# Attention, residual and layer norm over 64 row tiles on one core: the order of six pieces of work in the last five tile pairs is changed

## The reference

```python
q = heads(x @ Wq + bq); k = heads(x @ Wk + bk); v = heads(x @ Wv + bv)
scores = einsum('bhqd,bhkd->bhqk', q, k) * scale
scores = where(mask == 0, -inf, scores)
out = einsum('bhqk,bhkd->bhqd', softmax(scores), v)
y = x + (out @ Wo + bo)
return (y - mean(y)) / sqrt(var(y) + 1e-5)
```

## Time and profile before

| what | us |
| --- | --- |
| median of 3 runs | 812.68 |
| lowest, highest | 810.5, 813.32 |
| the profiled execution | 811.64 |
| its span, first to last instruction | 809.5 |
| TensorE busy | 800.8 |
| VectorE busy | 642.8 |
| GpSimd busy | 551.4 |
| ScalarE busy | 267.1 |

### The profile page before, as it was taken

The page is one execution under the profiler, slowest core; times in us unless marked ns, Lnnn a source line. Parts: engine busy times, 40 slices in busy tenths (PEclk is TensorE's granted clock), DMA queues, the critical chain, the costliest instruction groups (busy, mean ns, idle before and its releaser), DMA issues.

```text
span 809.5 us, 26951 instructions
## 1 busy us (share of the span) xinstructions
PE 800.8 (99%) x11771; PEld 679.1 (84%) x11771; DVE 642.8 (79%) x1002; ACT 267.1 (33%) x349; POOL 551.4 (68%) x443
## 2 busy tenths in 40 slices
PE   9999999999999999999999999999999999999997
PEld 7778888888888888888888888888888888888876
DVE  5968778787778887887877788877878777876895
ACT  6533333323333223332233332233322333323223
POOL 1797778666687666786667767667866668755672
PEclk9999999999999999999999999999999999999999
DMA  9334545254352534534345344444435435234342
GB/s 330 125 80 121 162 119 160 84 154 142 106 183 79 161 118 119 177 98 142 115 114 177 115 129 124 146 146 117 156 88 163 122 116 176 75 105 117 96 107 103
DMA packets 64965, 106.62 MB, mean 132 GB/s; under 512 B 11728, under 2 KB 28624, under 8 KB 62672
## 3 DMA queue, kind: packets, MB, share of 16 engines
q1 hardware_dynamic: 52368, 87.85, 34.7%
q10 hardware_dynamic: 12480, 17.06, 8.1%
HBM read 54.53 MB, written 16.78 MB: 88 GB/s over the span
## 4 chain that ended last, share of the span: by engine, by line
PE 93%; DVE 2%; DMA 2%; POOL 1%; SPq 1%; issue 0%; ACT 0%; POOLq 0%; DVEq 0%
PE ring L367 15%; PE ring L369 14%; PE ring L368 14%; PE ring L519 7%; PE ring L520 7%; PE ring L523 7%; PE psum_s L470 6%; PE psum_s L440 6%; PE ring L461 6%; PE psum_s L472 6%; PE psum_s L474 6%; DMA x_raw<-in_xt 2%; DVE x_lo L885 0%; DVE wo_lo L1014 0%; POOL soft L232 0%; POOL soft L1178 0%
## 5 line engine op out<-in xcount | busy, mean ns | idle before, releaser
L1178 POOL TENSOR_TENSOR soft<-soft,top 128x1024 f32<-128x1024 f32 x62 | 123.4, 1991 | 22.1 <-DVE top L950 22.1
L232 POOL TENSOR_TENSOR soft<-soft,inverse 128x1024 f32<-128x1024 f32 x62 | 118.8, 1918 | 25.9 <-DVE inverse L957 25.8
L954 DVE TENSOR_REDUCE total<-soft 128x16 f32<-128x1024 f32 x62 | 75.2, 1213 | 48.8 <-ACT soft L713 48.8
L367 PE MATMUL ring<-x_hi,wk_hi 128*128 128x512 f32 x256 | 103.2, 403 | 1.6 <-DVE v L891 1.3
L713 ACT ACTIVATE soft<-soft 128x1024 f32<-128x1024 f32 x62 | 65.8, 1062 | 111.6 <-POOL soft L1178 111.6
L369 PE MATMUL ring<-x_hi,wk_lo 128*128 128x512 f32 x256 | 99.9, 390 | 0.0
L368 PE MATMUL ring<-x_lo,wk_hi 128*128 128x512 f32 x256 | 99.7, 389 | 0.0
L519 PE MATMUL ring<-wo_hi,ot_hi 128*128 128x512 f32 x252 | 99.1, 393 | 0.0
L520 PE MATMUL ring<-wo_lo,ot_hi 128*128 128x512 f32 x252 | 98.9, 392 | 0.0
L748 ACT CAST s_hi<-v 128x1024 fp32r<-128x1024 f32 x27 | 28.3, 1047 | 207.4 <-DVE v L903 207.4
L367 PE MATMUL ring<-x_hi,wq_hi 128*128 128x512 f32 x248 | 96.6, 389 | 0.0
(11 more groups left out here) (125 smaller groups left out, 1878.2 us busy)
## 6 DMA issues: line engine op xcount, KB each, us to landing
pt<-soft SPq DMA_DIRECT2D x248, 64.0 KB, 2.5
x_raw<-in_xt SPq DMA_DIRECT2D x15, 1024.0 KB, 6.8
row<-in_x SPq DMA_DIRECT2D x60, 256.0 KB, 2.7
out_rows<-row SPq DMA_DIRECT2D x60, 256.0 KB, 2.4
pt<-soft ACTq DMA_DIRECT2D x232, 64.0 KB, 2.3
v<-in_xt SPq DMA_DIRECT2D x27, 512.0 KB, 4.6
adj<-in_adj SPq DMA_DIRECT2D x16, 128.0 KB, 2.7
kt<-in_wk SPq DMA_DIRECT2D x4, 256.0 KB, 5.7
```

The lines of the kernel that those rows point to most:

```text
L232: ops.tensor_tensor(soft_of(c), soft_of(c), on_keys(inverse[:, c % 2, :]), ALU.mult).then_inc(normed, 1)
L367: nc.tensor.matmul(out, left_hi, right_hi, start=kc == 0, stop=False)
L954: nc.vector.tensor_reduce(total[:, c % 2, :], by_row_head(soft_of(c)), AX_XY, ALU.add).then_inc(summed, 1)
L1178: nc.gpsimd.tensor_tensor(soft_of(c), soft_of(c), on_keys(top[:, c % 2, :]), ALU.subtract).then_inc(centred, 1)
```

## The change

Five orders change in the tail, and one pair's copies are divided.

- PE: `project_out(T-10)` now runs ahead of the scores of T-6 and T-5, not behind them.
- ACT: `read_q(T-1)` and `read_k(T-1)` go from behind `norm_by_act(T-10)` to behind the first and the second of the two exponentials.
- ACT and SP: `SHARED` now holds all tiles. The copies of T-4 and T-3, all sixteen issued by SP before, are issued half by SP and half by ACT. ACT's first four stand between `exp(T-3)` and `exp(T-2)`, its other four between `exp(T-2)` and `read_ot(PAIRS-3)`.
- DVE: `add_row(T-10)` goes ahead of `mask(T-6)`, and `read_v(T-8)` between the two masks.
- DVE: `turn(T-3)` goes from behind `mask(T-2)` and `add_y(T-7)` to ahead of both.

```diff
-SHARED = (*range(TILES - 4), TILES - 2, TILES - 1)
+SHARED = range(TILES)
 # PE
+            pe.wait_ge(ot_lo_done, PAIRS - 4)
+            project_out(T - 10)
             score(T - 6)
             score(T - 5)
-            pe.wait_ge(ot_lo_done, PAIRS - 4)
-            project_out(T - 10)
             pe.wait_ge(k_done, T - 1)
             project_v(T - 8)
 # ACT
             exp(T - 6)
+            read_q(T - 1)
             exp(T - 5)
+            read_k(T - 1)
             norm_by_act(T - 10)
-            read_q(T - 1)
-            read_k(T - 1)
             place(T - 6)
             place(T - 5)
...
             exp(T - 4)
             exp(T - 3)
+            place(T - 4)
             exp(T - 2)
+            place(T - 3)
             read_ot(PAIRS - 3)
             exp(T - 1)
             place(T - 2)
 # DVE
+            add_row(T - 10)
             mask(T - 6)
+            read_v(T - 8)
             mask(T - 5)
-            add_row(T - 10)
-            read_v(T - 8)
             sum_up(T - 6)
...
             read_v(T - 5)
+            turn(T - 3)

             mask(T - 2)
             add_y(T - 7)
-            turn(T - 3)
             mask(T - 1)
```

## The result

| | kernel before | kernel after |
| --- | --- | --- |
| median of 6 runs | 812.06 us | 818.18 us |
| lowest to highest | 809.64 to 813.32 | 814.52 to 819.45 |
| profiled execution, its span | 811.64, 809.5 | 814.52, 812.7 |
| ratio after to before | | 1.0062, 95% interval 1.004 to 1.0084 |

The change makes the kernel slower: by 5.0 us by the ratio (interval 3.2 to 6.8) and by 6.1 us by the medians. The forecast was +1.2. The profiled execution of after is the fastest of its six runs (four of the others took 817.85 to 819.45) and only 2.9 us slower than the profiled one of before, so the profile shows at most the mechanism and not the whole size of the loss.

The account below looks back on a forecast made before the run. TensorE was taken to bound the kernel. Extras of 1.51 us hidden in waits (0), project_out(T-8) 0 and project_out(T-6) +1.2 gave 812.68 + 1.2 = 813.9 us; range 810.9 to 816.0.

Parts of the forecast that it names:

- the wait ahead of `project_out(T-6)`: TensorE near the tail's end: starts at 780.2 instead of 778.99, 1.2 us late, the whole forecast loss.
- TensorE's pace: The tail runs at TensorE's pace; any order can gain at most the bursts' extra time, 1.51 us.
- The exchange: Output projection of T-10 ahead of the scores of T-6: scores end at 740.7, not 738.2, softmax 2.5 us late.
- The copies of T-6: SyncE's last copy issued at 755.6, landing 2.0 us later at 757.6, so mask(T-4) starts at 757.65, 0.9 late.
- `project_out(T-8)` at 763.85, nothing lost: First narrow place: VectorE's two masks and split run to 763.8, so TensorE starts at 763.85; change against before 0.
- The third rival: Store and copies each landing in 3.2 us put mask(T-4) at 760.0, 3.2 late; +3.55 us, 816.2; chance 0.15.
- turn(T-3) ahead: VectorE: the turn adds some 1.2 us ahead of mask(T-2), which starts at 770.7, 1.55 late.
- The second narrow place just holds: Ahead of mix(T-6): add_y(T-7) is done at 773.85 and the mix comes at 773.85 to 773.9.
- The issues ahead of `read_ot(PAIRS-3)`, +1.2: ScalarE: four issues of T-3 take 2.5 us behind exp(T-2), hold the readout to 777.85 and project_out(T-6) by 1.2.
- By that rule the division would be worth nothing and cost nothing: Copies on two engines: the skill's rule calls issue time usually small, giving no change; the forecast held the CAST at 733.74 against it.
- The second rival: Tail's slow bursts vanish and no wait replaces them: gain of up to 1.5 us, 811.2; chance 0.18.
- the extras of the bursts: TensorE's tail: two score bursts and a mix run 0.19, 0.45 and 0.87 us long, in all 1.51.

Follow-up runs that it names:

- e2: Kernel before with only the copies of T-4 and T-3 divided over SyncE and ScalarE; 810.5 us, ratio 0.9995 to before.
- e15: e3 with x_raw as softmax buffer of T-4 and T-3, the old buffer for T-2 and T-1; 810.78 us, ratio 0.9998 to before.
- e13: Kernel after without three quarters of the score matmuls of T-4, T-3 and tile 20; 814.0 us, ratio 1.0044 to before.
- e14: Kernel after with SyncE's copies of T-6 and T-5 ahead of row T-10's store and row T-6's load; 820.19 us, ratio 1.011 to before.
- e1: Kernel before with only turn(T-3) moved ahead of mask(T-2); 812.88 us, ratio 1.0019 to before.
- e6: e1 with 32 small matmuls ahead of the warm-up, itself cut from nine to six matmuls; 815.06 us, ratio 1.0047 to before.
- e8: e2 with 32 small matmuls ahead of the warm-up, itself cut from nine to six matmuls; 815.94 us, ratio 1.0059 to before.
- e10: Kernel after with x_raw as softmax buffer of T-4 and T-3, plus 120 semaphore increments on TensorE early in the loop; 814.14 us, ratio 1.0034 to before.
- e5: Kernel before with 32 small matmuls ahead of the warm-up, itself cut from nine to six matmuls; 814.82 us, ratio 1.0042 to before.
- e9: Kernel after with 32 small matmuls ahead of the warm-up, itself cut from nine to six matmuls; 820.12 us, ratio 1.011 to before.
- e3: Kernel after with T-4 and T-3 copies all on SyncE and turn(T-3) at its old place; 814.52 us, ratio 1.0041 to before.

## Why the prediction was wrong

The step that failed is the one on the copies of T-6: the landing behind the last issue was put at 2.0 us and measured 4.47, and a wait put at nothing ahead of `project_out(T-8)` measured 3.2. What was forecast as the loss, the wait ahead of `project_out(T-6)`, was not there. That a loss was forecast and a loss came is luck: the term that was forecast isn't the one that came.

- *TensorE's pace, and no more than 1.5 us to gain:* nothing speaks against it. No kernel of the study beats before; the best, e2 and e15, equal it.
- *The exchange delays the scores of T-6 by 2.5 us, mask(T-6) at 740.9, mask(T-5) at 744.3:* right to 0.1.
- *The copies of T-6:* here it failed. The step reads "the last at 755.6, and land 2.0 later, 757.6". The issue was right to 0.1, the landing 2.5 us off. I took the median "since this stretch moves little else"; it moved the row's load and the 16 KB of a fetch behind the scores of T-4, which account for about 0.6 and 1.9 us (the first share only suggested by e13 and e14). A second wait, 1.0 us for T-5's copies ahead of `mask(T-3)`, was in no sum.
- *`project_out(T-8)` at 763.85, nothing lost:* wrong in consequence, 767.4, and 1.7 us of half clock behind it were in no sum. The forecast had left VectorE's chain 0.05 us of slack there.
- *The third rival* was this mechanism, with `mask(T-4)` at 760.0; it came at 760.1. It had a chance of 0.15, and a price of +3.55 at `project_out(T-6)`. The wait took its price one block earlier, and the rival lacked the half clock behind it, 1.7 us. It wanted two long landings; the store's was as laid out (2.06 us to the load), and one, of the copies, was enough.
- *turn(T-3) ahead:* costed at 1.2 us on VectorE and nothing on TensorE. e1 has 1.5 us, with a longer stop inside the mix, which e6 takes away. "The second narrow place just holds" was right, as a wait for VectorE there is in neither e1 nor after, but by the table of nine kernels the margin that the turn used up was what kept the stop short.
- *The issues ahead of `read_ot(PAIRS-3)`, +1.2:* the mechanism is right, as e8 and e10 show (0.9 and 2.1 us), but with the copies' division alone it is hidden behind the stop in the mix (e2: nothing). In the profiled execution of after it costs nothing beyond the wait ahead of it.
- *"By that rule the division would be worth nothing and cost nothing":* with the rule of DMA: Bandwidth & Descriptors in the Trainium skill, section "Issuing engines are not separate DMA queues", e2 agrees (no difference), e8 doesn't (a tail 0.93 us longer than that of e5, from the division alone).
- *The second rival, the extras of the bursts:* the one in the mix goes when the blocks end elsewhere (e5), so it is a late fetch, but its removal gave nothing back at the end.

Open: four of six executions of after were 3 to 5 us slower than the profiled one. Their spans, first to last instruction, were only 1.8 to 3.8 us longer than its 812.7; the rest lies outside the instructions. The profile of e9 (after, shifted), with both waits in it, suggests that these pay the forecast's term too; no profile of such an execution of after was had. That the trailing updates are those of the one DMA engine that does the fetch is inferred from their equal steps and from the table, not seen; the packets' engines are not in the trace.

## What to carry to other kernels

A buffer that is reused as soon as its copies land has the landing's tail in the path: take the worst landing beside the fetches and transfers that will then be under way, not the median of a quiet stretch, and see first whether another buffer is free (e15). Where the bound engine has half a microsecond to spare at each of several places, a chain that moves by one or two microseconds must be priced with the state behind the wait too, since 3.2 us of standing cost up to 1.7 more in clock. And a burst of many small instructions behind a semaphore that is released late can run into the end of its instruction block.

## What the runs showed of the hardware

- A fetch of 16 KB of TensorE's instructions beside DMAs of 64 KB let their last updates come 1.3 to 2.0 us after the rest in seven of eight kernels (tile T-6); without a fetch 0.1 to 0.3 in eight.
- A burst of 256 instructions behind a wait stopped for 0.8 to 1.1 us with 1.3 to 1.9 us between release and start, and for 2.1 to 2.5 us with under 0.5 (nine kernels).
- Four DMA issues of 64 KB took ScalarE's sequencer 2.4 to 3.1 us, and the readout behind them waited for them though its data was there.
- After a stand of 3.2 us (after) or 2.4 us (e9) the granted clock was 0.5 for 3.4 us, which cost 1.6 to 1.7 us; after one of 1.6 us (e3) it stayed up.
- With 32 small matmuls in place of three large ones in the warm-up the full clock came at 12.1 to 13.9 us (e5, e6, e8, e9) and not at 5.4, and e5 and e6 took 4 us longer.
